# Perceiver stack, decoder layers: cross-attention scores of two sequences in eight array tiles and four PSUM banks, with their transposes in the same banks

## The reference, cut to what matters

```python
for l in range(6):
    x = ln(x + mha(x, x, sa_w[l], sa_b[l], mask))        # 16 heads of 16, 32 keys
    x = ln(x + mha(x, ctx, ca_w[l], ca_b[l], None))      # 16 heads of 16, 257 keys
    x = ln(x + relu(x @ w1[l] + b1[l]) @ w2[l] + b2[l])  # 256 -> 1024 -> 256
```

## Time and profile before

| | us |
|---|---|
| median of 3 runs | 4497.27 |
| lowest, highest | 4491.02, 4501.04 |
| the profiled execution | 4490.38 |
| its span, first to last instruction | 4488.6 |
| TensorE matmul busy in the span | 3979.4 (89%) |
| VectorE, ScalarE busy | 2618.1 (58%), 1875.0 (42%) |
| decoder scores, first to last start | 773.8 to 2691.1 |

### The profile page before, as it was taken

The page is one execution under the profiler, slowest core; times in us unless marked ns, Lnnn a source line. Parts: engine busy times, 40 slices in busy tenths (PEclk is TensorE's granted clock), DMA queues, the critical chain, the costliest instruction groups (busy, mean ns, idle before and its releaser), DMA issues. The chain is left out here.

```text
span 4488.6 us, 103588 instructions
## 1 busy us (share of the span) xinstructions
PE 3979.4 (89%) x43122; PEld 2985.1 (67%) x43122; DVE 2618.1 (58%) x5484; ACT 1875.0 (42%) x5200; POOL 299.8 (7%) x560
## 2 busy tenths in 40 slices
PE   7988995999999999999999997687688778789867
PEld 6766984677777777777777775576455577466535
DVE  3445114777777777777777765501477545255535
ACT  2221221445445545455545453122466445156523
POOL 0000101000000000000000000101111000000000
PEclk9998997999999999999999999799799788889878
DMA  4110583001111111111011000066444200100000
GB/s 151 60 59 3 187 298 119 30 27 50 52 43 35 52 45 33 61 40 59 30 51 57 21 20 10 36 259 250 150 148 153 68 0 0 35 29 20 11 1 12
DMA packets 116915, 310.46 MB, mean 69 GB/s; under 512 B 29352, under 2 KB 75624, under 8 KB 92016
## 3 DMA queue, kind: packets, MB, share of 16 engines
q1 hardware_dynamic: 113392, 295.61, 19.2%
q0 software_dynamic: 3072, 8.39, 0.5%
HBM read 289.01 MB, written 14.94 MB: 68 GB/s over the span
## 5 line engine op out<-in xcount | busy, mean ns | idle before, releaser
L2524 ACT COPY layers_pT<-banks 128x512 f32<-128x512 f32 x384 | 227.2, 592 | 554.3 <-PE banks L2292 553.6
L2223 PE MATMUL banks<-weights_a,ctx_tiles 128*128 128x256 f32 x1536 | 363.8, 380 | 0.0
L2216 PE MATMUL banks<-ctx_tiles,weights_a 128*128 128x512 f32 x768 | 363.5, 596 | 0.0
L2517 ACT ACTIVATE layers_probs<-banks,layers_negmax 128x256 f32<-128x256 f32 x768 | 354.1, 480 | 14.0 <-DVE layers_negmax L2382 6.8
L2223 PEld LDWEIGHTS banks<-weights_a,ctx_tiles 128*128 128x128 f32 x1536 | 285.8, 191 | 75.9 <-issue 46.4
L2360 DVE TENSOR_TENSOR layers_V<-banks,rows_a 128x512 f32<-128x512 f32 x192 | 132.8, 692 | 221.0 <-PE banks L2223 217.1
L2292 PE MATMUL banks<-const,layers_probs 128*128 128x128 f32 x1536 | 244.6, 282 | 2.8 <-ACT layers_pT L2524 2.8
L2292 PEld LDWEIGHTS banks<-const,layers_probs 128*128 128x128 f32 x1536 | 171.5, 141 | 106.5 <-issue 96.6
L2381 DVE TENSOR_REDUCE layers_negmax<-banks 128x4 f32<-128x1024 f32 x192 | 234.0, 1219 | 3.9 <-PE banks L2284 3.9
L2484 ACT ACTIVATE layers_KT<-banks,layers_less_last 128x256 f32<-128x256 f32 x384 | 162.1, 480 | 157.2 <-PE banks L2216 157.1
L2284 PE MATMUL banks<-layers_KT,layers_qblk 32*64 32x256 f32 x3072 | 211.3, 389 | 0.0
(11 more groups left out here) (702 smaller groups left out, 8435.0 us busy)
## 6 DMA issues: line engine op xcount, KB each, us to landing
ctx_tiles<-in_ctx SPq DMA_DIRECT2D x65, 1028.0 KB, 5.1
weights_a<-in_L_w SPq DMA_DIRECT2D x44, 1024.0 KB, 5.3
l2x_B<-positions SPq DMA_DIRECT2D x32, 1280.0 KB, 5.9
weights_b<-in_L_w SPq DMA_DIRECT2D x32, 1024.0 KB, 6.1
weights_c<-in_L_w SPq DMA_DIRECT2D x16, 1024.0 KB, 7.1
weights_b<-in_L_xattn_w SPq DMA_DIRECT2D x12, 1024.0 KB, 7.4
l0x_key_rows<-in_ctx_rows SPq DMA_DIRECT2D x32, 256.0 KB, 2.6
ctx_tiles<-in_ctx_keys SPq DMA_DIRECT2D x32, 256.0 KB, 2.7
```

The source lines that it names most:

```text
L2216: last = mm(o.rearrange("p (j k) -> p j k", j=2), ca_wk[:, c, m * P:(m + 1) * P], keys, start=c == 0, stop=c == DC - 1)
L2223: last = mm(o[:, b * D:(b + 1) * D], E.ctx[:, tile % 2, c, first:first + P], ca_wv[:, c], start=c == 0, stop=c == DC - 1)
L2517: a(probs[:, cc, i, t], ps[:, t, i % 2 * KW:(i % 2 + 1) * KW], ACT.Exp, bias=negmax[:, cc, t, i:i + 1], accum_out=totals[:, cc, t, i:i + 1 ...
L2524: nc.scalar.copy(pT[:, k % 4].rearrange("p t c x -> p (t c x)"), ps[:, TURN]).then_inc(s["copied"], 1)
```

## The change

A pair's scores move from banks 0 and 1 to the lower halves of banks 0 to 3, and its eight score matmuls each get an array tile of their own: which 64 columns a row group uses (`side`) now depends on the sequence's parity too. The pair's transposes go to the upper halves of the same four banks, all eight in a row, at a place that the table `TURN_AT` names inside the pair's own odd unit (before: four in each of the two units after the exponentials' own). `PV` becomes bank 4, and the ring has three banks, 5 to 7. The scores of a pair now wait until the transposes of the pair before are copied (before: until its exponentials were done). In `UNIT_JOBS`, `S1k` goes ahead of `S1q` and `K1`, `D2` from u6 to u5, and `V3` from u5 to u6. ScalarE copies a pair's transposes in the odd unit ahead of `K1` (u1), ahead of `D2` (u5), or at the end (u3, u7).

```diff
-    TURN, PV, RING, RB = 2, 3, 4, 4
+    PV, RING, RB = 4, 5, 3
+    TURN_AT = {1: ("behind", "S1q"), 3: ("behind", "K"), 5: ("behind", "D2"), 7: ("within", "D3")}
...
-        [("S1q", None, "dve"), k_job(1), ("S1k", None, "act"), ("n", None, "act")],
+        [("S1k", None, "act"), ("S1q", None, "dve"), k_job(1), ("n", None, "act")],
...
-        [("D1", 0, "act"), v_job(3), ("S6", None, "dve")],
-        [("D2", 1, "act"), ("X", None, "act")],
+        [("D1", 0, "act"), ("D2", 1, "act"), ("S6", None, "dve")],
+        [v_job(3), ("X", None, "act")],
...
-                    need(pe, "exp_done", 2 * k)
+                    need(pe, "copied", k)
+                    for r in range(4):
+                        for a in range(2):
+                            side = (r + a) % 2
+                            rows, half = slice(32 * r, 32 * (r + 1)), slice(64 * side, 64 * (side + 1))
+                            last = mm(ps[half, 2 * a + r // 2, 0:KW], qblk[rows, tile % 2, cc, j + a], KT[rows, tile % 2, cc, (j + a) * KW:(j + a + 1) * KW], start=True, stop=True)
+                    last.then_inc(s["scores_done"], 1)
+
+                def transposes(k, pos, cc, j):
+                    pe.wait_ge(s["exp_done"], 2 * (k + 2))
                     for a in range(2):
-                        for r in (0, 2, 1, 3):
-                            rows, half = slice(32 * r, 32 * (r + 1)), slice(64 * (r % 2), 64 * (r % 2 + 1))
-                            last = mm(ps[half, r // 2, a * KW:(a + 1) * KW], qblk[rows, tile % 2, cc, j + a], KT[rows, tile % 2, cc, (j + a) * KW:(j + a + 1) * KW], start=True, stop=True)
...
+                        for t in range(2):
+                            for c in range(KC):
+                                last = tr(ps[:, 2 * a + t, KW + c * P:KW + (c + 1) * P], probs[:, cc, j + a, t, c * P:(c + 1) * P], E.c("ident"))
+                        last.then_inc(s["transposed"], 1)
...
-                    if ca_unit(it - 2):
-                        transposes(*ca_unit(it - 2))
                     for a in jobs_in(it):
                         job(*a)
+                        turn(it, "behind", a[3])
+                    turn(it, "at the end", None)
...
+                    late = it % 2 and ca_unit(it)
+                    for i, b in enumerate(jobs_in(it)):
+                        if late and b[3] == {1: "K", 5: "D2"}.get(u):
+                            for back in (1, 0):
+                                copy_transposed(*ca_unit(it - back))
+                            late = None
```

More of the change, by code:

```diff
@@ L2271, in job @@
                         for m in range(FC):
+                            if m == FC // 2:
+                                turn(step * U + u, "within", kind)
                             last = mm(o[:, 0:D], hid[:, m], dm_w2[:, m], start=m == 0, stop=m == FC - 1)
@@ L2279, in scores, with turn @@
                         need_evacuated(pe, pos, "K", (DC - 1, 1))
-                    need(pe, "exp_done", 2 * k)
-                    for a in range(2):
-                        for r in (0, 2, 1, 3):
-                            rows, half = slice(32 * r, 32 * (r + 1)), slice(64 * (r % 2), 64 * (r % 2 + 1))
-                            last = mm(ps[half, r // 2, a * KW:(a + 1) * KW], qblk[rows, tile % 2, cc, j + a], KT[rows, tile % 2, cc, (j + a) * KW:(j + a + 1) * KW], start=True, stop=True)
+                    need(pe, "copied", k)
[4 more added lines that the diff above has]
+                            last = mm(ps[half, 2 * a + r // 2, 0:KW], qblk[rows, tile % 2, cc, j + a], KT[rows, tile % 2, cc, (j + a) * KW:(j + a + 1) * KW], start=True, stop=True)
                     last.then_inc(s["scores_done"], 1)
                 def transposes(k, pos, cc, j):
-                    need(pe, "exp_done", 2 * (k + 1))
-                    need(pe, "copied", k)
-                    for t in range(2):
-                        for c in range(KC):
-                            last = tr(ps[:, TURN, (KC * t + c) * P:(KC * t + c + 1) * P], probs[:, cc, j, t, c * P:(c + 1) * P], E.c("ident"))
-                    last.then_inc(s["transposed"], 1)
+                    pe.wait_ge(s["exp_done"], 2 * (k + 2))
+                    for a in range(2):
+                        for t in range(2):
+                            for c in range(KC):
+                                last = tr(ps[:, 2 * a + t, KW + c * P:KW + (c + 1) * P], probs[:, cc, j + a, t, c * P:(c + 1) * P], E.c("ident"))
+                        last.then_inc(s["transposed"], 1)
+                turned = set()
+                def turn(it, where, kind):
+                    if it % 2 and ca_unit(it) and it not in turned and (TURN_AT[it % U] == (where, kind) or where == "at the end"):
+                        transposes(*ca_unit(it - 1))
+                        turned.add(it)
                 def values(k, pos, cc, j):
@@ L2303, in values @@
                         for i in range(4):
-                            last = mm(ps[32 * i:32 * (i + 1), PV, j * 64:(j + 1) * 64], V[:, pos % 2, KC * j + c, cc * P + 32 * i:cc * P + 32 * (i + 1)], pT[:, k % 4, i // 2, c, 64 * (i % 2):64 * (i % 2 + 1)], start=c == 0, stop=c == KC - 1)
+                            side = (i + j) % 2
+                            last = mm(ps[32 * i:32 * (i + 1), PV, j * 64:(j + 1) * 64], V[:, pos % 2, KC * j + c, cc * P + 32 * i:cc * P + 32 * (i + 1)], pT[:, k % 4, i // 2, c, 64 * side:64 * (side + 1)], start=c == 0, stop=c == KC - 1)
                     last.then_inc(s["pv_done"], 1)
@@ L2307, in values @@
                         pe.wait_ge(s["spread_ready"], k // GB + 1)
-                        for i in range(4):
-                            last = mm(ps[32 * i:32 * (i + 1), PV, D:2 * D], E.c("headcol")[:, 32 * (i % 2):32 * (i % 2 + 1)], spread[:, i // 2].rearrange("p s j q -> p (s j q)"), start=True, stop=True)
+                        for a in range(2):
+                            for i in range(4):
+                                side = (i + a) % 2
+                                last = mm(ps[32 * i:32 * (i + 1), PV, D:2 * D].rearrange("p (s i a q) -> p s i a q", s=2, a=2, q=LQ)[:, :, :, a], E.c("headcol")[:, 32 * side:32 * (side + 1)],
+                                          spread[:, i // 2].rearrange("p s (i a) q -> p s i a q", a=2)[:, :, :, a], start=True, stop=True)
                         last.then_inc(s["shares_done"], 1)
@@ L2523, in copy_transposed @@
                     need(act, "pv_done", k - 3)
-                    nc.scalar.copy(pT[:, k % 4].rearrange("p t c x -> p (t c x)"), ps[:, TURN]).then_inc(s["copied"], 1)
+                    nc.scalar.copy(pT[:, k % 4].rearrange("p t c x -> p t (c x)"), ps[:, k % 2 * 2:k % 2 * 2 + 2, KW:2 * KW]).then_inc(s["copied"], 1)
                 for it in range(N * U):
@@ L2535, in _ @@
                         exponentials(*ca_unit(it))
-                    for b in jobs_in(it)[early:]:
-                        take(*b)
+                    late = it % 2 and ca_unit(it)
[4 more added lines that the diff above has]
+                            late = None
+                        if i >= early:
+                            take(*b)
+                    if late:
+                        for back in (1, 0):
+                            copy_transposed(*ca_unit(it - back))
                     if steps[step]["sa"] is not None and u == 3:
```

6 lines of the change are left out of this document (2 added, 4 removed).

## The result

| | median, us | lowest, highest | runs |
|---|---|---|---|
| before | 4500.25 | 4487.42, 4506.02 | 13 |
| changed | 4509.96 | 4505.31, 4518.13 | 13 |

The ratio of the two is put at 1.0026, with a 95% interval of 1.0017 to 1.0034; the medians differ by 9.7 us. The change makes the kernel slower by about a quarter of a percent, some 10 us. The profiled execution of the changed kernel took 4505.31 us with a span of 4503.5.

The account below looks back on a forecast made before the run. TensorE's order of work was taken to set the decoder's time. +0.20 a step over 42 steps (+8.4), -1 for steps with `X` and +5 at the start made +12 on the 4497.3 median: 4509, forecast 4500 to 4520, range 4474 to 4545.

Parts of the forecast that it names:

- first steps: Decoder steps 1 and 2: `V3` no longer covers `S6`'s wait, and step 2's transposes await their own exponentials; +5 for both.
- score burst: Each pair's scores on TensorE: two rounds on eight tiles, 0.63 us, 0.40 saved four times a step, -1.60.
- `D2` waits for `K3`: With three ring banks, TensorE's `D2` waits for ScalarE's evacuation of `K3`: chain 8.94 against work 7.66, +1.28 a step.
- transposes in `D3`: Fourth pair's transposes inside `D3` wait for their exponentials: 7.50 after `S6` began against work 6.89, +0.61 a step.
- `S1q` waits for `K0`: `S1q` waits for `K0`'s evacuation, 5.43 after the scores against work of 5.23: +0.1 a step, between 0 and 0.2.
- `D3`'s old wait ends: `D3` no longer waits for `D2`'s evacuation, so `S7` holds TensorE 0.86 in place of 1.05: -0.19 a step.
- an ordinary step: Sum of the burst's gain, the new waits and the ended wait: +0.20 a step, 42 steps, +8.4.
- steps with `X`: Five steps where `X`'s 0.8 us in front of `D3` cover the second wait: -0.2 each, so -1.
- at no cost in itself: Moved transposes, L2309's matmuls, maxima over more banks and copies were priced at nothing.
- scores stay at four tiles: Rival: bursts keep 1.03 while the waits shrink, +0.9 a step, 4544 us; half-way about 4525; chance 0.18.
- the chain is shorter: Rival: chain from `V2` to `K3` under 8.94; 0.25 off makes the run level, all 1.28 off gives 4449; chance 0.15.
- The third rival: The wait of the transposes in `D3` is smaller or absent, hiding 0.3 a step: 4490 at most; chance 0.15.

Follow-up runs that it names:

- e1: Changed kernel with the scores back on four array tiles, banks, ring and job order kept: 4551.10 us, ratio 1.0113 to before.
- e2: Changed kernel with ScalarE evacuating `K3` ahead of the exponentials in unit 4: 4460.28 us, ratio 0.9911 to before.
- e3: Changed kernel with the fourth pair's transposes behind six of `D3`'s eight products in place of four: 4489.83 us, ratio 0.9977 to before.
- e4: Changed kernel with both `K3` evacuated ahead of the exponentials and the transposes later in `D3`: 4429.53 us, ratio 0.9854 to before.
- e6: Kernel before the change with only a ring of three banks, the eighth bank idle: 4576.11 us, ratio 1.0206 to before.
- e7: Kernel before the change with only the new order of jobs, four ring banks kept: 4472.24 us, ratio 0.9969 to before.
- e5: The kernel of e4 with the old order of jobs in steps 0 to 2: 4418.07 us, ratio 0.9841 to before.

## Why the prediction came out right, and where its terms were off

The forecast was 4509, slower, and 4509.96 was measured. Its sum was +12 on the median, and it came to about +10. The mechanism is right: a shorter burst, taken back by the two waits that the prediction names. That the sum fits to 2 us is luck. The ordinary steps, priced at +8.4, gave +3.7, the first steps came to the forecast figure for other reasons, and the tail, which made up for it, was not priced.

| term | predicted, us | measured in the trace | |
|---|---|---|---|
| score burst | 0.63, -1.60 a step | 0.61 to 0.62, -1.64 | right |
| `D2` waits for `K3` | +1.28 | 1.20, and 0.11 longer `D2` | right |
| transposes in `D3` | +0.61 | 0.44, and 0.05 | too large |
| `S1q` waits for `K0` | +0.1 | 0.03 | too large |
| `D3`'s old wait ends | -0.19 | -0.25 | a little small |
| other jobs behind the scores | not priced | +0.15 | missing |
| an ordinary step | +0.20 | +0.09 | |
| steps with `X` | -0.2 | -0.08 | |
| first steps | +5 | +5.3, and 1.2 ahead of `K0` | right in size, not in its parts |
| last steps | not priced | -1.3, and +3.2 to +6.6 in the tail | missing |

**The burst.** The bounds were 0 and 0.43 saved. The prediction took two rounds on eight tiles in place of four rounds on four, and 0.41 to 0.42 was saved. Two row groups write one bank in the same round, in different halves of its partitions, and the sixteen are through in 0.69. By the rule of the Trainium skill (TensorEngine Tiling, Restrictions and Gotchas), that different row tiles cannot access the same PSUM bank at the same time, the burst should have stayed near 1.0; the trace disagrees with it as worded, at 0.69 for the sixteen. e1 shows that it is the tiles and not the banks: with the same four banks and four tiles it is 1.09. The rival "scores stay at four tiles" would have given 4544, and e1, which makes it true by hand, gives 4551.

**The two waits.** Both stand where the walk put them, with the releasers named. The chain from `V2` to `D2` was put at 8.94 and is 8.86, so the rival "the chain is shorter" has 0.08 of the 0.25 that it needed to reach the level of before. Up to the end of `K3`'s evacuation it is not shorter at all: 8.81, and 8.80 in the rows before. `D2` only follows faster, 0.05 behind that end, where I took 0.14. On the other side stands a cost that I had not counted: behind its wait `D2` holds TensorE 1.89 in place of 1.78, and the transposes 0.93 in place of 0.88. I put this down to the first weight load, which no matmul ahead hides; that is a reading. e2 and e3 take the waits away one at a time and get back 1.27 and 0.51, which are the waits with these extra times (1.31 and 0.49). So the cause is shown for the ordinary steps: what the bursts gain, these two waits take back.

**The third rival,** "the second wait is smaller or absent", was right in kind: 0.44 in place of 0.61, or 0.49 with the 0.05 behind it. The transposes too follow 0.05 and not 0.14 behind their release, and the work ahead of them was 6.95 and not 6.89.

**What failed in the ordinary steps** is the sentence that the transposes are moved "at no cost in itself". They had stood behind the scores and were 0.05 longer there; the jobs that follow the scores now, `q` and `V3`, and `K2`, which has lost the transposes ahead of it too, pay 0.10 each. Rows of e4 give 0.99 for the first job behind the scores of u2, where `S1k`'s kind of eight matmuls takes 0.89. Three places at 0.05 are 0.15, and with it the terms add up: -1.64 + 1.31 + 0.49 + 0.03 - 0.25 + 0.15 = +0.09, the 40.52 against 40.43. The reading is from rows and was not isolated by a run, and that the array mode is the cause is not shown.

**The ring.** The prediction took the ring of three as the source of the waits but did not say what it costs by itself. e6 and e7 do: three banks in the old order cost 1.94 a step, the new order with four banks gains 0.26. The reordering is what makes a ring of three bearable at all; what it leaves of the price is `D2`'s wait.

**The first steps.** Measured: +0.4 from `K0` to the first scores, +6.5 in step 2, -1.6 in step 3: +5.3. From the decoder's first matmul to its first `K0` it takes 1.2 more, which the prediction did not price. The distances from scores to scores show where step 2 grows:

| step 2, us | u0, u1 | u2, u3 | u4, u5 | u6, u7 | all |
|---|---|---|---|---|---|
| before | 9.40 | 9.84 | 9.17 | 6.88 | 35.29 |
| changed | 11.99 | 10.03 | 12.66 | 7.07 | 41.75 |

The prediction named two causes, `V3`'s cover missing in front of `S6` and the fourth pair's transposes waiting for their own exponentials. The first does not lengthen step 2, since `S6` starts as long after the third scores as before (7.25, 7.26; see e5). The second is seen, 1.68, but u6 and u7 grow by 0.19 only. The growth stands elsewhere. In u0 and u1 `S1q` waits for `K0`'s evacuation, as this row of the changed kernel's TensorE timeline shows:

```profile
794.89 1.16 PE L2209 MATMUL banks<-layers_sa_nT,weights_c 128*128 128x128 f32 x8 [2.71 <-ACT layers_KT L2499]
```

This is the term put at 0.1 a step. It is 0.03 in an ordinary step and 2.87 here (`S1k` starts at 791.13 and takes 0.89, `S1q` starts at 794.89). In u4 and u5 the third pair's transposes come behind `S6` (1.03 in e5, at the full clock) where others had filled its wait, and 2.33 is clock: 5.41 for what takes 3.08 in e5.

**The tail is the term that was missing.** The last steps have no jobs to put between a pair's scores and its transposes. Before, the scores of the next pair waited only for the exponentials of the pair before, and ran ahead of its transposes, which had a bank of their own; now they wait for the copies, and so for transposes that stand right behind their own exponentials. The timeline of the changed kernel's last scores and transposes:

```profile
2692.30 0.69 PE L2288 MATMUL banks<-layers_KT,layers_qblk 32*64 32x256 f32 x16
2696.72 1.97 PE L2296 MATMUL banks<-const,layers_probs 128*128 128x128 f32 x8 [3.74 <-ACT layers_probs L2532]
...
2705.65 1.97 PE L2296 MATMUL banks<-const,layers_probs 128*128 128x128 f32 x8 [2.12 <-ACT layers_probs L2532]
...
2721.02 1.09 PE L2296 MATMUL banks<-const,layers_probs 128*128 128x128 f32 x8 [2.28 <-ACT layers_probs L2532]
```

From the last step's first scores to the decoder's end it is 61.68, and 55.12 before: +6.6. The other kernels narrow the cause down. With the new banks this stretch is 58.3 to 60.5 (e1 to e5). With the old ones it is 54.7 in e7, which has the new order, and 56.5 in e6, which has the ring of three. So the order is not the cause, the ring of three alone goes with 1.4, and the new banks, with the ring and the scores' new wait, go with 3.2 or more. That it is this wait is read from the rows; no run takes it away alone. A part is clock: behind the first wait the three groups up to the next scores take 3.77 (2696.72 to 2700.49) at a granted clock of 0.50, and 1.99 for the third pair (2713.87 to 2715.86).

Summed over the decoder, from `K0` to its end, the trace gives 1998.4 against 1984.7, +13.7. By the terms: 39 ordinary steps at 0.095 - 0.4 for those with `X` + 5.3 - 1.3 + 6.6 = 13.9. (The prediction counted 42 ordinary steps; three of these are the first two and the last, which have terms of their own.) The medians differ by 9.7, the two profiled executions by 14.9. Beside the decoder, the profile of after has TensorE's first matmul of it 11.4 us later (731.77, 720.36) and the part behind it 11.4 shorter. Both lie in code that the change does not touch, and the latter varies between 1749 and 1761 over all these profiles.

## What to carry to other kernels

A gain on an engine that is busy all the time is worth its full amount only if the engines behind it have that much slack: walk the chain that starts at the last point where the follower was idle, and compare it with the engine's own new work up to where it meets that chain again. A resource given up for a gain (a bank of the ring here) comes back as waits at particular jobs; name those jobs, and the repair is often the order in which another engine serves two requests (e2: one job ahead of four exponentials, 1.3 us of 40.5 a step). Price the first and the last rounds of a pipeline by themselves, term by term: the work that covers a new dependency in the middle is missing there (`S1q`'s wait, 0.03 in the middle and 2.87 in step 2), and behind such a wait the same work can take longer by the clock.

## What was not expected of the hardware

**Records of a matmul grow with eight tiles, though the burst shrinks.** All score matmuls of the changed kernel, by line (min/median/max ns, first and last start):

```profile
L2288 PE MATMUL banks<-layers_KT,layers_qblk x3072: 374/425/685, 786.8 to 2716.2; 32*64 32x256 f32 x192
```

The median is 425 ns, and 374 in the earlier trace rows. Sixteen of them took 1.09 us at the shorter duration and take 0.69 at the longer one: a matmul's mean duration says nothing about its pace when tiles overlap, only the distance between starts does.

**The clock falls in the tail.** The windows view of the changed kernel in the tail (columns as in the first such row; the granted clock is the 0.77):

```profile
2692.30:2715.00 22.70, 15.51 (x209) 11.80 (x206) 12.60 (x32) 10.14 (x36) 1.58 (x4) 0.77 0.00 1
```

In the middle of the decoder the granted clock is 1.00, the 2.4 GHz level. Here TensorE was busy for 15.51 of 22.70 us, waiting for exponentials in between, and the mean is 0.77, so part of the stretch ran at 1.2 GHz: the transposes behind the first two waits are recorded for 1.97, and for 1.09 behind the third. A wait in the tail thus cost more than its own length here.
